# A perceiver block on one Trainium2 core: points 15 apart in a sub-block, centre loads moved, value matmuls split off, mix ahead of scores

## The reference, cut to what matters

```
neigh  = gather(feats, inds)                       # 10 neighbours in each of 4 orders
gf     = concat([center, neigh - center])          # per order
x16    = allf.reshape(B * N, k, 256).astype(f16)   # 8 heads of 32
scores = einsum('bihd,bjhd->bhij', qh, qh) / sqrt(32)
out    = einsum('bhij,bjhd->bihd', softmax(scores), qh)
fused  = out @ W_lin.T + b_lin
h      = einsum('oc,bnkc->bonk', W_conv, fused)    # 32 outputs in layer 1, 64 in layer 2
feats1 = lrelu(instance_norm(h)).max(axis=k)
```

## Time and profile before

| | us |
|---|---|
| median of 3 runs (2703.09 to 2705.81) | 2704.42 |
| the profiled execution's own time | 2693.29 |
| its span | 2691.5 |
| gather_windows, layer 1 and 2 | from 181 and 977 on, to 378 and 1174 |
| window_attention, layer 1 and 2 | 378 to about 960, 1174 to about 1825 |

### The profile page before, as it was taken

One profiled execution on the slowest core, in us unless ns is written; L12 is line 12 of the kernel. 1 busy time (PEld: TensorE's weight loads), 2 busy tenths in 40 slices (PEclk: granted clock), 3 DMA queues, 4 the chain that ended last, 5 costly groups with the idle time before them and its releaser, 6 DMA issues. The chain is left out here.

```text
span 2691.5 us, 119989 instructions
## 1 busy us (share of the span) xinstructions
PE 1997.2 (74%) x48106; PEld 1420.5 (53%) x48106; DVE 1852.2 (69%) x4073; ACT 1381.4 (51%) x2858; POOL 778.7 (29%) x996
## 2 busy tenths in 40 slices
PE   0586636666666656648888888885789999999977
PEld 0124325556555634338888888883334544454432
DVE  7889975555555559964555555557758888888875
ACT  0489843333333359834555555554564555555532
POOL 0010023443444420033333333330024444444321
PEclk9996667777778765678999999997999999999988
DMA  1105665555555516654555554542022222222210
GB/s 51 12 6 133 150 152 113 130 127 127 129 128 129 126 43 151 149 128 109 115 111 115 115 115 112 117 105 80 25 86 78 90 77 79 82 82 78 82 55 18
DMA packets 494619, 263.01 MB, mean 98 GB/s; under 512 B 362667, under 2 KB 463947, under 8 KB 494408
## 3 DMA queue, kind: packets, MB, share of 16 engines
q1 hardware_dynamic: 489512, 257.92, 39.8%
q10 hardware_dynamic: 5024, 4.00, 0.6%
HBM read 208.85 MB, written 52.96 MB: 97 GB/s over the span
## 5 line engine op out<-in xcount | busy, mean ns | idle before, releaser
L872 PE MATMUL pQ<-QW,QX 128*30 128x42 f16 (+1 forms) x23040 | 709.3, 298 | 297.6 <-DMA QX<-scratch_q 264.0
L872 PEld LDWEIGHTS pQ<-QW,QX 128*30 128x30 f16 x23040 | 659.7, 142 | 323.9 <-issue 322.2
L981 POOL TENSOR_TENSOR Ap<-E,RM 128x450 f32<-128x450 f32 x384 | 371.9, 969 | 59.7 <-POOL RM L976 58.6
L1011 ACT ACTIVATE E<-Dm 128x150 f32<-128x150 f32 x384 | 125.9, 328 | 465.7 <-DVE Dm L938 465.5
L955 DVE TENSOR_REDUCE hmax<-Hs 128x450 f32 (+1 forms) x144 | 89.7, 623 | 325.1 <-ACT junk L1023 325.1
L976 POOL TENSOR_TENSOR RM<-R,own 128x45 f32<-128x45 f32 x384 | 100.5, 262 | 671.4 <-DVE R L944 671.0
L1016 ACT ACTIVATE Vs<-pQ 128x480 f32<-128x480 f32 (+1 forms) x384 | 292.5, 762 | 0.0
L928 DVE TENSOR_REDUCE mx<-pQ 128x15 f32<-128x150 f32 x384 | 116.4, 303 | 218.9 <-PE pQ L872 217.8
L949 DVE STREAM_TRANSPOSE AT<-Ap 128x480 f32<-128x480 f32 x384 | 244.6, 637 | 21.1 <-POOL Ap L981 19.6
L1969 POOL TENSOR_TENSOR MT<-cb,decay 128x512 f32 (+1 forms) x128 | 163.9, 1302 | 244.8 <-PEq L1737 147.9
L609 DVE TENSOR_TENSOR QT<-ext,cen 128x1650 f16<-128x1650 f32 x96 | 233.0, 2488 | 1.8 <-issue 1.5
(11 more groups left out here) (365 smaller groups left out, 3295.1 us busy)
## 6 DMA issues: line engine op xcount, KB each, us to landing
QW<-scratch_q SPq DMA_DIRECT2D x192, 240.0 KB, 3.0
QX<-scratch_q SPq DMA_DIRECT2D x576, 80.0 KB, 2.6
QX<-scratch_q SPq DMA_DIRECT2D x192, 240.0 KB, 3.4
scratch_q<-QT SPq DMA_DIRECT2D x120, 360.0 KB, 5.0
Wg<-in_in_proj SPq DMA_DIRECT2D x64, 256.0 KB, 2.7
Wh<-in_in_proj SPq DMA_DIRECT2D x64, 256.0 KB, 2.8
Wo<-in_out_proj SPq DMA_DIRECT2D x64, 256.0 KB, 2.6
W_s<-in_in_proj SPq DMA_DIRECT2D x16, 256.0 KB, 2.7
```

The costliest lines, as they stand in the source:

```text
L872: last = nc.tensor.matmul(pQ[32 * h:32 * h + PTS * K, p, u // PB, at0:at0 + ON], query, both, start=True, stop=True)
L981: nc.gpsimd.tensor_tensor(subs(A[:, p, :], 32)[:, :, 0:PTS * K].rearrange("p s (n j) -> p s n j", n=PTS), subs(E[:, p, :], K).unsqueeze(2) ...
```

## The change

1. Sub-blocks of points 15 apart: sub-block u of a tile now holds points u, u + 15 and u + 30. `QT` is read as (g n) runs of 15 neighbouring points; the subtraction is three instructions over 12, 12 and 10 such runs, one over the rest of 3 points, one over the first 6 points. The centre matmul and the maximum of the mix take the new order by their access patterns.
2. Centre loads: in layer 1 they go from SP's queue to ACT's, 4 tiles at a time, one step after the scores; in layer 2 they stay with SP, two tiles at a time, but for the pair 4 tiles back.
3. In layer 2 (WIDE is false) a sub-block's scores are 4 matmuls over 10 columns with 96 rows, into `pS`, and its values 4 matmuls over 64 columns straight from `W["stack"]`, which lie side by side, into `pV`; both sets load the query. `QW` shrinks to the keys, and the copies of weights into it go. Layer 1 keeps its matmuls of 42 columns.
4. PE's step has mix(k) ahead of scores(k).
5. The mix takes strips of O columns instead of 32: in layer 2, 15 x 2 strips of 64. In layer 1 nothing changes there.
6. `CT` is cleared by DVE instead of POOL; `hmax2` is allocated after the second gather.

```diff
 in gather_windows, DVE
-                    for n in range(PTS):
-                        v.tensor_tensor(QT[:, k, 0:LAST, n, :, 0:SUBS],
-                                        rows(ext, k, ahead + n, (GP, LAST), (1, K), (PTS, SUBS)),
-                                        rows(cen, k, n, (GP, LAST), (0, K), (PTS, SUBS)),
+                    runs_of = QT[:, k, :, :, :, :].rearrange("p g n j u -> p (g n) j u")
+                    for r0, r1 in zip(THIRDS, THIRDS[1:]):
+                        v.tensor_tensor(runs_of[:, r0:r1, :, 0:SUBS],
+                                        rows(ext, k, ahead + SUBS * r0, (SUBS, r1 - r0), (1, K), (1, SUBS)),
+                                        rows(cen, k, SUBS * r0, (SUBS, r1 - r0), (0, K), (1, SUBS)),
                                         ALU.subtract).then_inc(q_v, 1)
-                    v.tensor_tensor(QT[:, k, LAST, :, :, 0:REST], ...
+                    v.tensor_tensor(runs_of[:, WHOLE, :, 0:REST], ...
-                    v.tensor_tensor(QT[:, k, 0, :, :, 0:2], rows(ext, k, 0, (K, PTS), (1, K), (PTS * K, 2)),
+                    v.tensor_tensor(runs_of[:, 0, :, 0:LEAD + 1], rows(ext, k, 0, (1, K), (K, LEAD + 1)),
...
 in window_attention
+    WIDE = O == C
+    CU = (4, 2)[O // C - 1]
-        QW = sb("QW", [128, NU, UT * 4, ON * SW], F16)
-        CT = sb("CT", [128, NU, UT * GP], F16)
+        QW = sb("QW", [128, NU, UT * 4, (ON if WIDE else K) * SW], F16)
+        CT = sb("CT", [128, U * GP], F16)
-        pQ = ps("pQ", [128, 2, NB, 512])
+        if WIDE:
+            pQ = ps("pQ", [128, 2, NB, 512])
+        else:
+            pS, pV = ps("pS", [128, 2, 512]), ps("pV", [128, 2, 1024])
+        def load_centres(eng, at, k):
+
+            (t, r), w = at, k // CU
+            c16 = scratch["c16"].rearrange("p (v x) -> p v x", x=CU * GP)
+            eng.wait_ge(mixed, pack(r, k + CU - 1) + 1)
+            eng.dma_start(CT[0:2 * C, w * CU * GP:(w + 1) * CU * GP],
+                          c16[:, bass.ds(r * (U // CU) + w, 1), :].rearrange("p v x -> p (v x)")).then_inc(c_in[w], 16)
 SP's step
-                    if first:
-                        sp.wait_ge(ct_zeroed, 1)
-                    sp.wait_ge(mixed, pack(r, k + UT - 1) + 1)
-                    sp.dma_start(CT[0:2 * C, w, :], ...
+                if at(4) and (k - 4) % CU == 0 and not WIDE:
+                    load_centres(sp, at(4), (k - 4) % U)
 PE's scores
-                            last = nc.tensor.matmul(pQ[32 * h:32 * h + PTS * K, p, u // PB, at0:at0 + ON], query, both,
-                                                    start=True, stop=True)
+                            if WIDE:
+                                last = nc.tensor.matmul(pQ[to, p, u // PB, at0:at0 + ON], query[h], keys[h],
+                                                        start=True, stop=True)
+                            else:
+                                nc.tensor.matmul(pS[to, p, u * K:u * K + K], query[h][0:96], keys[h][0:96],
+                                                 start=True, stop=True)
+                        if not WIDE:
+                            for h in range(4):
+                                to = slice(32 * h, 32 * h + PTS * K)
+                                last = nc.tensor.matmul(pV[to, p, u * O:u * O + O], query[h], W["stack"][:, h, :],
+                                                        start=True, stop=True)
 PE's mix
-                    for w in range(first // UT, k3 // UT + 1):
-                        pe.wait_ge(c_in[w], r * 16 + 16)
+                    pe.wait_ge(c_in[first // CU], r * 16 + 16)
-                        for slot, half in strips:
-                            at0 = slot * O + 32 * half
-                            last = nc.tensor.matmul(pH[at0:at0 + 32, p, 32 * u:32 * u + PTS * K],
-                                                    Vs[:, (first + slot) % RV, u * O + 32 * half:u * O + 32 * half + 32],
+                        for slot in range(SL):
+                            last = nc.tensor.matmul(pH[slot * O:slot * O + O, p, 32 * u:32 * u + PTS * K],
+                                                    Vs[:, (first + slot) % RV, u * O:u * O + O],
                                                     AT[:, (first + slot) % NA, 32 * u:32 * u + PTS * K],
                                                     start=False, stop=u == SUBS - 1)
             def step(k, at):
+                mix(k, at)
                 scores(k, at)
-                mix(k, at)
 DVE, hmax
-                    v.tensor_reduce(hmax[:, bass.ds(q * GP, GP)],
-                                    Hs[:, p, :].rearrange("p (n j) -> p n j", j=K), X, ALU.max).then_inc(hmax_done, 1)
+                    v.tensor_reduce(hmax[:, bass.ds(q * GP, GP)].rearrange("p (n s) -> p s n", n=PTS),
+                                    Hs[:, p, :].rearrange("p (s n j) -> p s n j", n=PTS, j=K), X, ALU.max)\
+                        .then_inc(hmax_done, 1)
 ahead of the steps, on DVE, POOL and ACT
-            for k in range(1, U, 3):
+            for k in range(1, U if WIDE else 0, 3):
                 v.tensor_copy(*weights_of(k)).then_inc(placed[k // UT], 1)
 ACT's step
+                if at(1) and (k - 1) % CU == 0 and WIDE:
+                    load_centres(act, at(1), (k - 1) % U)
```

More of the change, by code:

```diff
@@ L774, in window_attention @@
         q_in = [sem(f"q_in{k}") for k in range(NU)]
-        c_in = [sem(f"c_in{k}") for k in range(NU)]
+        c_in = [sem(f"c_in{k}") for k in range(U // CU)]
         projected = sem("projected")
@@ L852, in _ @@
             none = A[:, 0:2, :].rearrange("p k x -> p (k x)").bitcast(F16)
-            for p in range(2):
-                for b in range(NB):
-                    nc.tensor.matmul(pQ[:, p, b, :], none[:, 0:128], none[:, 0:512], start=True, stop=True)
-            pe.wait_ge(rows_zeroed, 1)
+            if WIDE:
+                cells = [pQ[:, p, b, :] for p in range(2) for b in range(NB)]
+                pe.wait_ge(rows_zeroed, 1)
+            else:
+                cells = [pS[:, p, :] for p in range(2)] + [pV[:, p, 512 * b:512 * b + 512] for p in range(2) for b in range(2)]
+            for cell in cells:
+                nc.tensor.matmul(cell, none[:, 0:128], none[:, 0:512], start=True, stop=True)
             def scores(k, at):
@@ L860, in scores @@
                     (t, r), p, w = at(0), k % 2, k // UT
-                    if isinstance(t, int) and t < U and k % UT == 0:
+                    if WIDE and isinstance(t, int) and t < U and k % UT == 0:
                         pe.wait_ge(placed[w], UT)
@@ L881, in mix @@
                     pe.wait_ge(copied, q + 1)
-                    for w in range(first // UT, k3 // UT + 1):
-                        pe.wait_ge(c_in[w], r * 16 + 16)
-                    strips = [(slot, half) for slot in range(SL) for half in range(O // 32)]
-                    for slot, half in strips:
-                        at0 = slot * O + 32 * half
-                        out = pH[at0:at0 + 32, p, 0:GC].rearrange("p (s x) -> p s x", x=32)[:, :, 0:PTS * K]\
-                            .rearrange("p s (n j) -> p s n j", n=PTS)
-                        c0 = (first + slot) % UT * GP
-                        ctr = CT[:, (first + slot) // UT, c0:c0 + GP].rearrange("p (s n) -> p s n", n=PTS).unsqueeze(3)\
-                            .to_broadcast([128, SUBS, PTS, K])
-                        nc.tensor.matmul(out, W["center"][:, 32 * half:32 * half + 32], ctr, start=True, stop=False)
+                    pe.wait_ge(c_in[first // CU], r * 16 + 16)
+                    if isinstance(t, int):
+                        pe.wait_ge(ct_zeroed, 1)
+                    for slot in range(SL):
+                        for half in range(O // 32):
+                            at0 = slot * O + 32 * half
+                            out = pH[at0:at0 + 32, p, 0:GC].rearrange("p (s x) -> p s x", x=32)[:, :, 0:PTS * K]\
+                                .rearrange("p s (n j) -> p s n j", n=PTS)
+                            ctr = CT[:, (first + slot) * GP:(first + slot + 1) * GP].rearrange("p (n s) -> p s n", n=PTS)\
+                                .unsqueeze(3).to_broadcast([128, SUBS, PTS, K])
+                            nc.tensor.matmul(out, W["center"][:, 32 * half:32 * half + 32], ctr, start=True, stop=False)
                     pe.wait_ge(vs_ready, t + 3)
@@ L964, in _ @@
                 nc.gpsimd.memset(blank(w), 0.0).then_inc(zeroed[w], 1)
-            nc.gpsimd.memset(CT[:, :, :], 0.0).then_inc(ct_zeroed, 1)
-            for k in range(2, U, 3):
+            for k in range(2, U if WIDE else 0, 3):
                 nc.gpsimd.tensor_copy(*weights_of(k)).then_inc(placed[k // UT], 1)
@@ L990, in _ @@
             act.dma_start(own[:, :], io["own"]).then_inc(const_in, 16)
-            for k in range(0, U, 3):
+            for k in range(0, U if WIDE else 0, 3):
                 nc.scalar.activation(*weights_of(k), ACT.Copy).then_inc(placed[k // UT], 1)
```

(3 more changed lines are left out.)

54 lines of the change are left out of this document (29 added, 25 removed).

## The result

The changed kernel takes **2994.07 us** (median of 4 runs, 2986.02 to 3003.93) against 2703.76 us for the kernel before on the same chip (2693.46 to 2705.81, 4 runs): a ratio of 1.1084, 95% interval 1.104 to 1.1128. The forecast was 2356 us with a range of 2240 to 2550. It was wrong in sign.

The account below looks back on a forecast made before the run. Bounds taken: DVE in the gathers, late `QX` loads behind SP's wait in attention 1, PE 88% busy in attention 2. Savings of 180 + 137 + 5 + 26 = 348 us from 2704.4 gave 2356 us, range 2240 to 2550.

Parts of the forecast that it names:

- The value matmuls: Layer 2: separate key and value matmuls bring a pair of tiles from 6.53 to 5.1 us, saving 137 us.
- The mix in strips of 64: Layer 2: half the instructions, each load twice as wide; kept at 1.2 us, some 0.4 more if loads do not hide.
- Rival C: Layer 2: switching between 96 and 128 rows empties the array, 270 ns a round; 3595 us in all; chance 0.05.
- The cost of a sub-block: Layer 2 scores: key round 33 ns plus value round 65, about 100 ns; a tile's scores 1.5 us instead of 2.1.
- rival A: Layer 2: short matmuls have a floor, 175 ns a sub-block instead of 141, losing 55 us; 2548 us; chance 0.13.
- its ends: Layer 2 bounds: 181 us saved with SP as bound at 4.65 a pair; 55 lost at 175 ns a sub-block.
- The centre loads: Layer 1: off SP's queue, PE's wait for `QX` goes; 2.93 to 2.0 us a tile, saving 180 us.
- Two signs that it named for layer 1: Layer 1, if right: granted clock near 1.0 and DMA share 0.8 or more.
- Mix ahead of scores: Both layers: the mix fills the time in which scores would wait for `Vs`; nothing added to the saving.
- The gathers: Both gathers: DVE's subtraction gets cheaper, its batch falls from 10.78 to 8.9 us, saving 26 us.
- the sign named for ACT: Gathers, if right: ACT busy 99%.
- matmul pairs of layer 2 over 4.2 us: Layer 2: sign that the forecast is wrong, pointing to rival A or Rival C.

Follow-up runs that it names:

- experiment 3: Changed kernel, but layer 2 does the key and value matmuls of only 12 of the 15 sub-blocks: 2458.25 us.
- 4: Changed kernel with layer 2 unrolled over 4 tiles instead of 6 and two pair buffers instead of three, all output computed: 2557.06 us.
- 2: Kernel before with 30, 22 or 14 one-column matmuls more a tile in layer 2: 3170.0, 2907.7 and 2709.1 us.
- 9: Experiment 4 plus layer 2's mix in strips of 32 and DVE's maximum not waiting for ACT's square: 2444.73 us.
- 5: Changed kernel with layer 2's 74-column matmuls restored and its mix in strips of 32 again: 2481.41 us.
- 8: Experiment 6 with layer 1's centre loads back in SP's queue, behind the wait for the mix: 2545.24 us.
- 6: Experiment 5 with DVE's maximum over the mixed values no longer waiting for ACT's square; ACT's copy waits instead: 2422.22 us.
- 10: Experiment 6 with scores ahead of the mix in layer 1 only: 2405.93 us.
- 7: Experiment 5 with scores ahead of the mix again in both layers: 2478.04 us.

## Why the prediction was wrong, step by step

**The value matmuls (forecast -137, measured +442): the step that failed.** "The mix in strips of 64: half the instructions" was the only sentence in which instructions were counted, and only for the time that they take. That the six-tile body grows from 1486 to 1846, and that a loop must stay in PE's instruction memory to run at its own pace, was in no term and in no rival. The pair that the sum has at 5.1 us took 11.3 (2 x 5.67). Rival C came out on the slower side by another mechanism, the emptied array, and with another number; experiments 3 and 4 exclude it for 96 and 128 rows, since the same alternation runs at 117 ns a sub-block. The mechanism that decides is shown by two experiments from both sides: the kernel before becomes as slow by its loop size alone (2), and the changed work becomes fast in a smaller loop (4). What sets the size of the loss is the pace of the blocks: they come without a pause, nine a pass, in the changed kernel (34.0 us a pass) and in the kernel before with 30 matmuls more (35.1), though the two do different work. The fallen clock goes with it: PE stands still every few microseconds, the granted clock is 0.52, and the mix takes 3.06 us in place of 1.69. But the clock does not set the pass: in the second of these kernels it is 0.79, and the pass is no shorter. No run changes the clock alone.

The term was wrong by more than that. With a loop that stays, the same matmuls give 650.5 us for attention 2 (4), 2.5 less than before where 142 less were forecast, and 603.1 at best (9). The next two items say why, and with the loop over four tiles PE also waits some 0.6 us a pair (9).

The Trainium skill, Runtime: NRT & Kernel Launch, section Instruction fetch mechanics, says that TensorE's instruction memory takes 128 KiB, 2048 instructions, that it is filled in blocks of 16 KiB, 256 instructions, and that a taken branch to a target outside the pages then held forces a fetch. The 16 KiB are what the trace has. By the size alone 1846 instructions would fit; here they did not stay, nor did 1750. The Trainium skill also calls the cost of crossing a block mostly hidden, and in this loop it is not: an estimate from its 256 instructions and the 3.76 us measured is 14.7 ns an instruction, while a round of four loads and four matmuls here takes 60 ns, 7.5 an instruction, so that PE runs about twice as fast as it is fed. By the same 256 of the Trainium skill, the 1846 instructions of a pass are 7.2 blocks, fewer than the nine that come; what the others hold no run shows.

**The cost of a sub-block (forecast 33 + 65 ns, measured 117 in experiments 3 and 4).** The rounds of keys and of values start 60 ns apart, whether 10 or 64 columns follow. The value round was about right at 65; the key round, at 33, was priced by its columns. What holds it at 60 I take to be its four strided loads, at 15 ns each, since the mix's loads, without a step, start 10 ns apart (1.21 us for 120); no run separates loads from matmuls. So a tile's scores take 1.76 us, not 1.5. This bears out half of rival A: there is a floor, at 60 ns and not at 87. The rule that the prediction set beside it, from the Trainium skill's TensorEngine Tiling (Array Packing), section Instruction Overhead, that a matmul with one free column takes as long as one with 60, fits: ten columns cost what 64 do. If it is the loads that set the round, it is no test of the rule.

Two readings in this part of the prediction do not hold. It says that the four column groups do not run side by side, from four centre matmuls of 450 columns in 0.40 us; that row shows only that columns without a step are cheaper, 0.22 ns each where the scores pay 0.42, and under rival A the same text has the groups side by side. And what stands beside the scores in a pair is 0.35 + 1.2 + 0.5 = 2.05 us in the forecast but 1.85 in its ends: with 2.05, rival A loses 74 us and not 55, and comes to 2567, beyond the range.

**The mix in strips of 64 (forecast 1.2 us, measured 1.69).** "If loads hide" they did not. For the change of width 0.35 us was named, and some 0.3 was measured (the first load 0.46 us after the centre's instead of 0.14), but in the sum of a pair 0.35 stands once, as the centre's. Undoing this part alone is worth 72 us (5).

**The centre loads (layer 1, forecast -180, measured -107).** The mechanism was right: the wait for `QX` went and comes back when the loads do (8), which costs 122 us. What the term left out is what is late next. I listed PE, SP, the double buffer and DMA, and took the double buffer's delay, 1.8 us from scores to `Vs`, from a row in which DVE was not held up. DVE's queue also holds `hmax`, once in four tiles, and it waits for ACT's square. In the kernel before that wait stood in the shadow of the late loads: from 500 to 900 DVE stood 68.8 us at it, but PE only 1.9 us for `Vs`. Freed of it (6) a tile takes the 2.0 us of the forecast instead of 2.33, and with the order turned too (10) layer 1 is 182 us shorter than before, 4.3 us a pair for the whole block. That this equals the 180 of the forecast owes something to the two changes that it did not have. Two signs that it named for layer 1 failed with the term: the clock was 0.84, not near 1.0, and the DMA share 0.71, not 0.8. What the new order of the points does in layer 1 was not run by itself.

**Mix ahead of scores (forecast nothing).** Right in the sum (3 us) by luck, since two effects cancel: it costs 12 us in layer 1 and saves 9 in layer 2 (7).

**The gathers (forecast -26, measured -32).** Timeline of DVE, one batch to the next:

```profile
288.95 5.61 DVE L609 TENSOR_TENSOR QT<-ext,cen 128x1800 f16<-128x1800 f32 x3 [0.63 <-ACT ext L698]
...
298.70 2.04 DVE L609 TENSOR_TENSOR QT<-ext,cen 128x1800 f16<-128x1800 f32 x1 [0.71 <-ACT ext L698]
```

2.04 us for 1800 elements, where 2.05 was named; a batch in 9.75 us, with DVE waiting for ACT. The term holds, and so does the sign named for ACT, full in the middle of the gather.

The condition "matmul pairs of layer 2 over 4.2 us" did come true as a sign of error, but it pointed to rivals A and C; it could not tell a slow matmul from a missing one.

## What to carry to other kernels

Before a loop is given more instructions, count what one pass puts on PE, with a load and a matmul for each product and twice that for f32, and compare it with bodies that are known to stay; here 1654 did and 1750 did not, and the step from one to the other made the block 29% longer. In a profile it looks like this: the engine waits for "issue" in the middle of a group without a semaphore, all others wait for it, the instruction queue has blocks in steady state, and the clock has fallen. And when a wait is taken from an engine, look for the next one in each queue of the loop, also at instructions that run only every fourth time.

## What the runs showed of the hardware that was not expected

- The instruction blocks of 16 KiB arrive one every 3.76 us (changed) and 3.9 us (before + 30: 180 in 700 us), though each transfer takes about 1 us and data uses the DMA engines only 30% of the time.
- There is a case in between: with 1750 instructions the blocks come in every other pass only.
- Rounds of four strided loads of 30 columns and four short matmuls start 60 ns apart, 15 ns a load, at a granted clock of 0.5 (changed kernel, 1502.74 and 1502.80) as at 1.0 (experiment 3, 1302.02 to 1302.14).
- f32 strips of 64 columns are dearer than twice as many of 32: 1.69 against 1.2 to 1.4 us for the same products, and another 0.3 us at the change between the widths.
